# Placing the dense pieces anew over the steps of a fused attention and feed-forward kernel on Trainium2

## The reference, cut to what matters

```python
qkv = x @ w_qkv.T + b_qkv
q = rope(elu(q) + 1);  k = rope(elu(k) + 1)
attn = softmax(q @ k.T / 4) @ v                   # per batch and head, 1024 x 1024
y = layernorm(x + attn + conv3(v, w_lepe) + b_lepe)
h = relu(s0 * ([y, -y] @ pm1(k0))) * 2            # pm1: True -> 1, False -> -1
h = relu(s1 * (h @ pm1(k1))) * 2                  # 1024 x 1024
out = layernorm(y + s2 * (h @ pm1(k2)))
```

## Time and profile before

| | before |
|---|---|
| median of three runs | 2267.48 us |
| the profiled execution's own time | 2269.32 us |
| its span, first to last instruction | 2267.5 us |
| busy: PE, DVE, ACT, POOL | 94%, 74%, 65%, 40% |
| mean granted TensorE clock | 0.97 of full speed |
| DMA | 76.87 MB, mean 34 GB/s |

### The profile page before, as it was taken

How to read it: one execution, slowest core, us unless ns; L and a number is a source line. 1 busy time by engine, 2 the same in 40 slices (tenths; PEclk the granted TensorE clock), 3 DMA queues, 4 the chain that set the end, 5 groups by cost and what they waited for, 6 DMA issues and landing times.

```text
span 2267.5 us, 43445 instructions
## 1 busy us (share of the span) xinstructions
PE 2133.7 (94%) x17088; PEld 869.2 (38%) x17088; DVE 1685.9 (74%) x3018; ACT 1475.4 (65%) x2845; POOL 913.3 (40%) x522
## 2 busy tenths in 40 slices
PE   4788899999999999999999999999999999899997
PEld 2122323344343444334343443434443343334344
DVE  6957687878787877878777787868778787878243
ACT  3157578766677666866677666776668666776631
POOL 1228608560375406851185603853067601600000
PEclk8579899999999999999999999999999999999999
DMA  5001110011001110012000210011101110010000
GB/s 176 27 8 39 48 45 16 27 52 39 15 9 52 54 32 13 25 45 67 15 15 29 69 39 15 9 52 61 31 9 34 36 48 15 16 34 1 1 19 19
DMA packets 40140, 76.87 MB, mean 34 GB/s; under 512 B 14992, under 2 KB 19456, under 8 KB 36864
## 3 DMA queue, kind: packets, MB, share of 16 engines
q1 hardware_dynamic: 34752, 51.02, 7.9%
q0 software_dynamic: 5184, 23.07, 2.8%
HBM read 46.27 MB, written 25.17 MB: 32 GB/s over the span
## 4 chain that ended last, share of the span: by engine, by line
PE 81%; DVE 13%; ACT 4%; issue 1%; DMA 1%; POOL 0%; SPq 0%; ACTq 0%; POOLq 0%; DVEq 0%
PE unit_banks L656 24%; PE unit_banks L533 20%; PE o_bank L586 20%; DVE maxima L892 9%; PE unit_banks L613 5%; PE unit_banks L669 5%; PE unit_banks L624 3%; ACT probs L745 2%; PE unit_banks L601 1%; PE unit_banks L543 1%; PE unit_banks L564 1%; PE unit_banks L568 1%; DVE h0T L959 1%; ACT rows L812 0%; PE unit_banks L594 0%
## 5 line engine op out<-in xcount | busy, mean ns | idle before, releaser
L892 DVE TENSOR_REDUCE maxima<-unit_banks 128x1 f32<-128x512 f32 x2048 | 1308.6, 685 | 428.9 <-PE unit_banks L533 422.1
L745 ACT ACTIVATE probs<-unit_banks 128x512 f32<-128x512 f32 x2048 | 1116.0, 598 | 665.4 <-PE unit_banks L543 655.1
L533 PE MATMUL unit_banks<-k_stack,q_stack 48*128 48x512 f16 x2048 | 662.2, 394 | 61.8 <-DVE maxima L892 38.3
L543 PE MATMUL unit_banks<-q_stack,k_stack 50*128 50x512 f16 x2048 | 651.2, 389 | 1.9 <-ACT probs L745 1.7
L586 PE MATMUL o_bank<-probs,v_pair 128*32 128x256 f32 x8192 | 570.1, 391 | 3.1 <-issue 3.1
L656 PE MATMUL unit_banks<-h0T,w 128*128 128x512 f16 x2048 | 480.9, 380 | 0.0
L1217 POOL TENSOR_TENSOR attn<-o_rows_sb,rden 128x256 f32<-128x256 f32 x63 | 39.0, 618 | 923.2 <-DVE rden L905 912.6
L533 PEld LDWEIGHTS unit_banks<-k_stack,q_stack 48*128 48x128 f16 x2048 | 154.5, 94 | 597.8 <-DVE maxima L892 300.0
L586 PEld LDWEIGHTS o_bank<-probs,v_pair 128*32 128x32 f32 x8192 | 208.8, 109 | 308.7 <-issue 217.4
L656 PEld LDWEIGHTS unit_banks<-h0T,w 128*128 128x128 f16 x2048 | 186.5, 98 | 228.1 <-issue 38.6
L543 PEld LDWEIGHTS unit_banks<-q_stack,k_stack 50*128 50x128 f16 x2048 | 153.3, 94 | 16.1 <-ACT probs L745 11.4
(11 more groups left out here) (125 smaller groups left out, 1541.7 us busy)
## 6 DMA issues: line engine op xcount, KB each, us to landing
rows<-in_x POOLq DMA_DIRECT2D x8, 1024.0 KB, 7.6
xT_sb<-in_xT SPq DMA_DIRECT2D x8, 1024.0 KB, 14.2
q_stack<-q_scratch SPq DMA_DIRECT2D x128, 64.0 KB, 2.0
k_stack<-k_scratch SPq DMA_DIRECT2D x128, 64.0 KB, 2.0
out<-rows SPq DMA_DIRECT2D x8, 1024.0 KB, 4.1
q_scratch<-parts POOLq DMA_DIRECT2D x14, 512.0 KB, 3.3
k_scratch<-parts POOLq DMA_DIRECT2D x14, 512.0 KB, 3.3
q_stack<-q_scratch SPq DMA_DIRECT2D x128, 32.0 KB, 1.9
```

Of the source, the lines that this page charges most:

```text
L533: nc.tensor.matmul(units.out(unit), q_stack[row:row + STACK, r, t * P:(t + 1) * P], k_stack[row:row + STACK, r, half * 512:(half + 1) * 51 ...
L543: nc.tensor.matmul(units.out(unit), k_stack[row:end, r, kt * P:(kt + 1) * P], q_stack[row:end, r, half * 512:(half + 1) * 512], start=True ...
L745: nc.scalar.activation(probs[:, 2 * (kt % 2) + h, half * 512:(half + 1) * 512], units.out(unit), ACT.Exp, scale=exp_regs[2 * (n % PAIRS) + ...
L892: nc.vector.reduce_max(maxima[:, v // T % 2, h * T + t, half:half + 1], units.out(unit), AXIS_X)\
```

## The change

- **The deal.** In each batch: q's projections from step 6 (before 7), k's from step 32 (before 29; for batch 1's k, made in batch 0, from step 22), V's from step 50 (before 43). The bounds stand at steps 14 and 40 (before 12 and 35; in batch 0 at 14 and 28). The feed-forward pieces follow: `hT` 19 and 20, `L0` 22 to 25, `L1` 26 to 31 and 36 to 45, `L0` of the second half 46 to 49, `L2` 54 to 57, `L1` 58 to 69 and 74 to 77, `L2` 79 to 82 (steps over 63 lie in the next batch). Steps 14 and 21 have no piece but the bounds. The last `L1` unit of batch 6 goes into the tail.
- **Rings.** `S` (0, 1), `T` (2, 3), the rest (4, 5, 6) from the first step on.
- **Bounds.** DVE sums the four relu sums into one column (`join_sums`), and `head_bounds` does one matmul of each of its two kinds where it did four.
- **FFN constants.** The nine small ones and w0 are made by DVE before the row maxima of the start; w1 and w2 by ACT in 20 instructions, one a step from step 8 on. The second stage buffer moves from `attn` to `rows[1]`.
- **POOL's and SP's order.** From batch 1 on `elu`, rotation and split of k stand behind `normalise_o` of pair 3, and `ln_scales` of the FFN's layernorm behind pair 2; `load_x` behind pair 5. `store_out` goes from pair 3 to 5, `load_edges` and xT from pair 5 to 6. The copies of v and the second layernorm's statistics and normalisation move to later steps with the pieces.

```diff
-Q_AT, K_AT, V_AT, SCALE_AT = 7, 29, 43, (12, 35)
-STATS_AT = {**{6 + t // 2: (0, t - t % 2) for t in range(0, T, 2)}, 14: (1, 4), 16: (1, 6), 52 + 4: (1, 0), 52 + 6: (1, 2)}
-MOMENTS_AT = {10: 0, 17: 1}
-NORMALISE_AT = ({13: 0, 14: 2, 15: 4, 16: 6}, {20 + t: t for t in range(T)})
-COPY_V_AT = {3: 3}
+Q_AT, V_AT = 6, 50
+K_AT, SCALE_AT = {1: 22}, ({}, {1: 28})
+STATS_AT = {**{6 + t // 2: (0, t) for t in range(0, T, 2)}, 27: (1, 4), 29: (1, 6), 59: (1, 0), 61: (1, 2)}
+MOMENTS_AT = {10: 0, 31: 1}
+NORMALISE_AT = ({13: 0, 14: 2, 15: 4, 16: 6}, {37 + t: t for t in range(T)})
+COPY_V_AT = {3: (0, 1, 2, 3, 4, 7), 1: (7,), 5: (7,)}
+WEIGHTS_AT = 8
+def k_at(c):
+    return K_AT.get(c, 32)
+def scale_at(c, which):
+    return SCALE_AT[which].get(c, (14, 40)[which])
...
+LATE_UNITS = [("L1", TAIL - 1, 1, KF - 1), *out_units(TAIL - 1, 1)]
...
-    rings = {"S": (0, 1, 4), "T": (2, 3, 5), "": (6, 0, 1, 2, 3, 4, 5)}
+    rings = {"S": (0, 1), "T": (2, 3), "": (4, 5, 6, 0, 1, 2, 3)}
...
-    rings[""] = (6,)
+    rings[""] = (4, 5, 6)
...
-        if s == BATCH:
-            rings = {"S": (0, 1), "T": (2, 3), "": (4, 5, 6)}
...
-                if j == 3 and b >= 2:
+                if j == 5 and b >= 2:
                     store_out(b - 2)
-                if j == 5 and b < NB - 1:
+                if j == 6 and b < NB - 1:
                     load_edges(b + 1)
...
-                units.wait_read(pe, ("proj", unit[1], 2 * w + 1, 1))
+                pe.wait_ge(sums_joined, 2 * c + w + 1)
                 units.wait_free(pe, unit)
...
+                nc.tensor.matmul(bank[:, 0:1], same_head[:], total, start=True, stop=True, skip_group_check=True)
+                nc.tensor.matmul(bank[:, 1:1 + H], total.to_broadcast([P, P]), head_mask[:], start=True, stop=True,
+                                 skip_group_check=True).then_inc(units.full_sem(unit), 1)
...
+            def weights(i):
+                if i == 0:
+                    act.wait_ge(weights_ready, 11)
+                if i < 2 * KF:
+                    k, cols = i // 2, slice(i % 2 * 512, (i % 2 + 1) * 512)
+                    nc.scalar.activation(w1[:, k, cols], k1_u8[:, k, cols], ACT.Identity, bias=s_work[:, 2:3],
+                                         scale=s_work[:, 1:2])
+                else:
+                    k = slice(2 * (i - 2 * KF), 2 * (i - 2 * KF) + 2)
+                    nc.scalar.activation(w2[:, k], k2_u8[:, k], ACT.Copy, bias=-1.0, scale=2.0)
...
+            def join_sums(c, w):
+                units.wait_read(dve, ("proj", c, 2 * w + 1, 1))
+                nc.vector.reduce_sum(sums[:, w:w + 1], relu_sum[:, 2 * w:2 * w + 2, :], AXIS_XY).then_inc(sums_joined, 1)
...
                 normalise_o(n + 2)
+                if b >= 2:
+                    ln_scales(b - 2, 1)
+                if b > 0:
+                    normalise_o(n + 3)
                 if b + 1 < NB:
                     elu(b + 1, 1)
                     rotate_side(b + 1, 1)
-                normalise_o(n + 3)
+                if b == 0:
+                    normalise_o(n + 3)
                 if b + 1 < NB:
                     split(b + 1, 1)
+                normalise_o(n + 4)
+                normalise_o(n + 5)
+                if b + 1 < NB:
                     load_x(b + 1)
-                for k in range(4, PAIRS - 1):
-                    normalise_o(n + k)
+                normalise_o(n + 6)
```

More of the change, by code:

```diff
@@ L316, in build @@
         relu_sum = sb("relu_sum", [P, 4, 2], F32)
+        sums = sb("sums", [P, 2], F32)
         pow2_q = sb("pow2_q", [P, 1 + H], F32)
@@ L554, in head_bounds @@
             def head_bounds(unit):
-                w = unit[2]
+                _, c, w = unit
                 pe.wait_ge(dve_setup, 3)
-                units.wait_read(pe, ("proj", unit[1], 2 * w + 1, 1))
+                pe.wait_ge(sums_joined, 2 * c + w + 1)
                 units.wait_free(pe, unit)
[L560 to L569, removed]
-                                            skip_group_check=True)
-                done.then_inc(units.full_sem(unit), 1)
+                bank, total = units.out(unit), sums[:, w:w + 1]
+                nc.tensor.matmul(bank[:, 0:1], same_head[:], total, start=True, stop=True, skip_group_check=True)
+                nc.tensor.matmul(bank[:, 1:1 + H], total.to_broadcast([P, P]), head_mask[:], start=True, stop=True,
+                                 skip_group_check=True).then_inc(units.full_sem(unit), 1)
             def weighted_v(s, half):
@@ L841, in _ @@
                     copy_o_rows(n - 1)
-                if kt == 3 and n > 0 and j != 5 and n + 3 < NB * PAIRS:
-                    copy_v(n + 2 if j == 6 else n + 3)
-                if kt == 5 and j == 6 and n + 3 < NB * PAIRS:
-                    copy_v(n + 3)
+                if n > 0 and j in COPY_V_AT.get(kt, ()):
+                    ahead = {1: 1, 3: 2, 5: 3}[kt] if j == PAIRS - 1 else 3
+                    if n + ahead < NB * PAIRS:
+                        copy_v(n + ahead)
                 for unit in done_within(s):
@@ L868, in _ @@
             copy_o_rows(NB * PAIRS - 1)
+            high_part(LATE_UNITS[0])
             for t in range(T // 2):
                 normalise(NB - 1, 0, t)
-            for unit in END_UNITS:
+            for unit in END_UNITS[len(LATE_UNITS):]:
                 if unit[0] in HIDDEN:
@@ L1026, in rotated @@
                     elu(0, 1 + ops[0] // 2)
+                if ops[0] == 4:
+                    join_sums(0, 1)
                 dve.wait_ge(start_split, ops[0])
@@ L1040, in _ @@
             v_out(("V", 0, 3))
-            for v in range(T + LEAD):
-                if v == T + 1:
-                    split_max_rows(0)
-                for h in range(2):
-                    for half in range(2):
-                        row_max(v, h, half)
-                if v == T - 1:
-                    join_maxima(0)
             dve.wait_ge(k_loaded, 6 * 16)
@@ L1069, in _ @@
                                                 ALU.mult, ALU.mult))
-            def weights(i):
-                if i == 0:
-                    then(nc.vector.tensor_tensor(w0[:], k0_u8[:, 0:KC], k0_u8[:, KC:2 * KC], ALU.subtract))
-                    then(nc.vector.tensor_scalar(w0[:], w0[:], s_work[:, 0:1], None, ALU.mult))
-                elif i <= 4:
-                    k = slice(2 * i - 2, 2 * i)
-                    then(nc.vector.tensor_scalar(w1[:, k], k1_u8[:, k], s_work[:, 1:2], s_work[:, 2:3],
-                                                 ALU.mult, ALU.add))
-                else:
-                    then(nc.vector.tensor_scalar(w2[:], k2_u8, 2.0, -1.0, ALU.mult, ALU.add))
+            then(nc.vector.tensor_tensor(w0[:], k0_u8[:, 0:KC], k0_u8[:, KC:2 * KC], ALU.subtract))
+            then(nc.vector.tensor_scalar(w0[:], w0[:], s_work[:, 0:1], None, ALU.mult))
+            for v in range(T + LEAD):
+                if v == T + 1:
+                    split_max_rows(0)
+                for h in range(2):
+                    for half in range(2):
+                        row_max(v, h, half)
+                if v == T - 1:
+                    join_maxima(0)
             for s in range(STEPS):
@@ L1095, in _ @@
                         split_max_rows(unit[1])
+                for w, at in enumerate((Q_AT, k_at(b + 1))):
+                    if b + 1 < NB and i == at + 5:
+                        join_sums(b + 1, w)
                 if kt == RECIPROCAL_STEP and n > 0:
@@ L1119, in _ @@
                         join_maxima(v // T)
-                if s < 6:
-                    weights(s)
+            for unit in done_behind(STEPS - 1):
+                dense(unit)
             final, m = NB * PAIRS - 1, NB - 1
@@ L1149, in _ @@
             ln_moments(m, 0)
-            for unit in END_UNITS[:2]:
+            for unit in LATE_UNITS:
                 dense(unit)
-            units.wait_read(dve, END_UNITS[1])
+            units.wait_read(dve, LATE_UNITS[-1])
             normalise(0)
@@ L1156, in _ @@
             ln_moments(m - 1, 1)
-            for unit in END_UNITS[2:]:
+            for unit in END_UNITS[len(LATE_UNITS):]:
                 dense(unit)
```

47 lines of the change are left out of this document (26 added, 21 removed).

## The result

Four runs of the changed kernel took 2223.43 to 2228.98 us, with a median of 2225.7; four of the kernel before had a median of 2266.13 us. The ratio is 0.9825, with a 95% interval of 0.9801 to 0.9849. The profiled execution took 2223.43 us, its span 2221.6. The forecast was 2221.

A forecast was written before the change was run, and what follows sets the result against it. PE bounds steps with a dense piece, DVE's and ACT's turnover of banks the others. Terms -41 - 8.5 - 25 + 5 + 20 + 3 = -46.5 from 2269.3 give 2222.8; median 1.8 lower, 2221 us; range 2192 to 2248.

The forecast's parts named there:

- Batch 0 and the start: Start and first batch: constants moved -11, pieces -50, scores' banks +14, conversions +6, in sum -41 us.
- the 52 other steps get two banks: Batch 0's steps without a piece: two banks for scores instead of three, 0.27 us each, +14 us.
- The rings: Batch 0: three banks for pieces and cheaper bounds save 50 us; fewer banks for scores cost 14.
- ScalarE's conversions: Batch 0, steps 8 to 27: ACT's 20 conversions at 0.6 us each, +6 us (0 to 14).
- Steady batches: Batches 2 to 6: bounds, bank waits and L0 places save 5.0 us each, -25 us in all.
- The bounds term 2.8: Each steady batch: a quarter of the bounds matmuls saves PE 2 x 1.42 = 2.8 us.
- New tight spots: Steady batches, steps 19 and 46: second unit takes a bank DVE frees only in that step, +0.7 us.
- Batch 1: Batch 1: 48 pieces instead of 51, the same bounds and L0 gains, -8.5 us (-4 to -11).
- Batch 7 and tail: Last batch and tail: one more piece +1, late L1 unit ahead of L2 +4 (0 to 6), together +5 us.
- The stall at step 48: Batches 1 to 6: PE waits 3.4 us (0 to 8) for row maxima queued behind k's stacks, +20 us.
- the clock, +3: Half rate of PE's clock behind some of the pauses at step 48, +3 us (0 to 20).
- the rival of no stall: Step 48: POOL's chain ends in time or SP is quicker; -23, 2198 us; chance 0.17.

The follow-up runs named there:

- e1: Changed kernel, but SP issues the row maxima of a batch's pair 6 ahead of the wait for k's scratch and the eight stack DMAs; 2210.41 us.
- e5: Changed kernel, but the start's scores before step 0 go round four banks (0, 1, 2, 3); 2214.96 us.
- e3: Changed kernel with the old bank rings in the start and batch 0 (three for each kind of scores, one for the rest); 2239.51 us.
- e4: Kernel before with only the new rings (two banks for each kind of scores, three for the rest from the first step); 2249.21 us.
- e6: Changed kernel, but ScalarE makes all 20 parts of w1 and w2 before its first exponential; 2215.21 us.
- e9: Changed kernel with the edits of e1, e5, e6 and e8 together; median 2194.16 us against 2267.83 for the kernel before, ratio 0.9682.
- e7: Changed kernel, but the bounds are again made by four matmuls of each kind from the relu sums, DVE's joined sum kept; 2231.84 us.
- e8: Changed kernel, but in the tail DVE takes the late L1 unit's low part between the halves of the first layernorm's statistics; 2218.61 us.
- e2: Changed kernel, but from batch 1 on POOL does k's ELU ahead of the division of pair 3; 2220.07 us.

## Why the prediction was right, and where its terms were off

The total was 4.7 us from the median and the mechanism foretold was the one found, but two errors of some 10 us each cancelled in it, and that they did is luck. e1, which has no stall, separates them: its span is 58.9 us below before's, where the terms without stall and clock came to 69.5; and the stalls are 13.0 us of the span (14.8 in the batches themselves), where stalls and clock were put at 23.

- **Batch 0 and the start, -41 expected.** With the start it was -35.2. Batch 0 ended near the 207 named (208.7), its pieces at 4.0 us, the small constants hidden at 0.15 to 0.17 each. On these last the Trainium skill ("SBUF — State Buffer", "SBUF: two separate sides") and the trace agree: with GpSimd idle, no small instruction took more than 0.17 us. **What failed was a missing term:** the step "the 52 other steps get two banks" was priced for steps only, and the start's 48 row maxima lost the third bank as well, at half clock and on the path. It cost 4.0 us (4.1 from first to last row maximum), and in e5 the row maxima have their old pace again.
- **The rings, -50 + 14 expected.** e3 and e4 give -20.7 and -25.2 for the two together. By e3's steps the +14 was near (+11.2), and the -50 was the mis-sized term: the steps with a piece give -31.9. That term had taken all that was left of batch 0's excess, and part of it went with the other edits (18.4 us, of which steps 0 to 5 give 15.4 where -11 was named). The sum of the parts held, its split did not.
- **ScalarE's conversions, +6 expected, 0 to 14.** e6 measured 6.6 in batch 0. That the number fits is luck: 2.7 us is the conversions' own (e9 against e5, steps 8 to 27), most of the rest came with the clock, which had not been in this term. One takes 0.826 us and not 0.6, or 11.38 / 16 = 0.71 from one to the next in e6. The Trainium skill's estimate ("ScalarE: Activation LUTs", "Rules for kernel authors") of 0.73 each is the nearer to that; but the +9 made of it, like the +6, is well above the conversions' own 2.7. ACT seems to have had more slack in these steps than both sums gave it.
- **Steady batches, -5.0 each expected.** Without stalls they are 258.5 (e1) against 263.0: -4.6 (the 263.0 is every one before but batch 3, which was 1.6 longer). The bounds term 2.8 has 1.34 of 1.42 shown by e7 at step 40. New tight spots cost more than 0.7: step 46, whose second `L0` unit takes a bank that DVE frees late (PE pauses 0.78 us there), is 4.88 us in place of 3.93. The other parts of the -5.0 were not undone one by one.
- **Batch 1, -8.5 expected.** -8.55 in e1; -4.1 with its stall.
- **Batch 7 and tail, +5 (0 to 6 in the late unit).** It was +7.4: 1.8 up to the last scores, where 1 was named, and 5.7 behind them, where 4 was. The low part behind the statistics is there, 2.72 us; e8 gives 2.9 back. The rest was not taken apart.
- **The stall at step 48, +20, and the clock, +3.** Right in place, cause and number (six, batches 1 to 6). The size of an undisturbed one was 1.35 us, not 3.4: the maxima landed at 54.6 instead of 55.8, and 13 steps take 53.2 instead of 52.4, as steps 40 and 46 are longer than an ordinary one. Batches 1 and 5 were 4 to 5 us because of one long issue each on SP and half clock behind. Both ends of this lay in the range kept (0 to 8), and the rival of no stall needed only 1.4 us less. So batches 2, 3, 4 and 6 take 259.8 to 260.0 us and batch 5 263.4, and none the 261 to 262 named. The expectation of e2 failed on the same chain: I had taken POOL's queue to be the anchor and had not looked at when k's last projection is there.

## What to carry to other kernels

When work is moved, follow each item that stands behind it in the same queue, SP's too: the stacks that were moved were in time themselves, and the four small DMAs behind them held PE; ordering them first (e1) gave 13 us for a move of three lines. When a buffer is taken from one use, price it in every phase that has that use, the prologue too, where the clock was low here and nothing overlapped. And don't book a gain on one of two causes that a row shows together: undo each alone, as e3 and e4 did, before the split is believed.

## What the runs showed of the hardware

- Some DMA issues on SP took 0.9 to 2.1 us where their like take 0.42. They come at nearly the same places of the program in the runs of different kernels: in batch 1's stacks in e1, e2, e3, e5, e6, e8 and e9 too (1.30 to 1.57 us), in batch 5's 1.15 to 1.40. e7, whose program has 192 more matmuls for the bounds, is the exception: batch 1's long issue (1.24 us) stands behind the maxima there, and batch 5's stacks have none. They go with the program, then, and not with chance; what causes them was not tested.
- A pause or a thin stretch of PE of a few us was followed by the granted clock at half (0.5) for 3.4, 6.8 or 10.2 us: after the stalls of batches 1 and 5, in steps 11 to 13 of batch 0, at e7's bounds, in the tail. With stalls of 1.35 to 1.6 us in the full steps of batches 2, 3, 4 and 6 there was none. Length alone doesn't decide it: behind pauses of 2.17 and 2.28 us in e6 (batches 1 and 5) the clock stayed full, and behind one of 1.96 in e2 (batch 1) it fell. What it costs can be read off batch 5: a pause of 2.3 us with 6.8 us of half clock behind it made the batch 4.9 us longer in the changed kernel, and a like pause with none 2.3 in e6.
